# Turning the quantized inputs by transposing DMA transfers in nine of the first eleven batches

## What is computed

```python
r_t = 0.9 * r_(t-1) + ctx_t * ctx_t              # a scan over the 512 rows of a batch
x = x + layernorm(x) * r
y = layernorm(x)
xq, s1 = quant_act_uint8(y)                      # one scale, from the maximum over all 32 batches
h = relu(xq @ quant(w1).T + b1)                  # 512 -> 2048
hq, s2 = quant_act_uint8(h)                      # again one scale over everything
x = x + (hq @ quant(w2).T + b2)                  # 2048 -> 512
```

## Time and profile before

| | |
|---|---|
| median of 3 runs | 1227.15 us (1222.93 to 1229.25) |
| the profiled execution, its own time | 1226.19 us |
| its span (first to last instruction) | 1224.0 us |
| TensorE busy | 1150.7 us, 94% |
| ScalarE busy | 950.9 us, 78% |
| VectorE busy | 870.7 us, 71% |
| moved by DMA | 448.72 MB, mean 367 GB/s |
| mean granted clock of TensorE | 0.978 of full |

### The profile page before, as it was taken

The page is one execution under the profiler, slowest core; times in us unless marked ns, Lnnn a source line. Parts: engine busy times, 40 slices in busy tenths (PEclk is TensorE's granted clock), DMA queues, the critical chain, the costliest instruction groups (busy, mean ns, idle before and its releaser), DMA issues.

```text
span 1224.0 us, 14776 instructions
## 1 busy us (share of the span) xinstructions
PE 1150.7 (94%) x5194; PEld 524.1 (43%) x5194; DVE 870.7 (71%) x1273; ACT 950.9 (78%) x1191; POOL 153.0 (13%) x400
## 2 busy tenths in 40 slices
PE   6888988886999999999999999899999999999998
PEld 2333333323444555444444444344444444444443
DVE  6999889985777897777777777555565555655565
ACT  5888978995777777777777775788888888888784
POOL 4455645551000110000000000000000000000000
PEclk9899889997999999999999999899999999999999
DMA  9999999922778999999999978799999999999996
GB/s 391 395 401 398 386 385 401 405 100 104 313 292 322 400 425 414 377 356 359 351 352 354 354 325 334 300 349 416 424 424 423 423 424 425 422 424 423 424 424 248
DMA packets 63570, 448.72 MB, mean 367 GB/s; under 512 B 6900, under 2 KB 6920, under 8 KB 9480
## 3 DMA queue, kind: packets, MB, share of 16 engines
q1 hardware_dynamic: 51976, 363.89, 72.7%
q10 hardware_dynamic: 11520, 83.89, 18.4%
HBM read 254.81 MB, written 192.94 MB: 366 GB/s over the span
## 4 chain that ended last, share of the span: by engine, by line
PE 79%; DMA 7%; ACT 6%; DVE 4%; issue 3%; POOL 1%; SPq 0%; ACTq 0%; DVEq 0%; POOLq 0%
PE ps L929 36%; PE ps L975 36%; DMA xq<-in_ctx_dram 6%; PE ps L901 3%; ACT xq L536 2%; PE ps L951 2%; ACT xq L525 2%; PE ps L893 1%; DVE work L680 1%; ACT xq L533 1%; DVE work L696 1%; DMA xq<-in_x_dram 1%; DVE xq L690 0%; ACT work L533 0%; ACT w1T L542 0%
## 5 line engine op out<-in xcount | busy, mean ns | idle before, releaser
L929 PE MATMUL ps<-xq,w1T 128*128 128x512 f16 x2048 | 449.5, 380 | 1.4 <-DVE xq L777 1.4
L975 PE MATMUL ps<-w2T,xq 128*128 128x512 f16 x2048 | 445.2, 380 | 2.3 <-ACT xq L638 2.0
L768 DVE TENSOR_REDUCE work<-xq 128x2 f32<-128x1024 f32 x255 | 309.8, 1219 | 116.6 <-ACT xq L582 116.6
L638 ACT ACTIVATE xq<-xq,hb,hs 128x512 f16<-128x512 f32 x446 | 321.0, 801 | 67.9 <-PE ps L975 58.9
L582 ACT ACTIVATE xq<-ps 128x1024 f32<-128x1024 f32 x255 | 260.9, 1023 | 126.9 <-PE ps L929 126.7
L975 PEld LDWEIGHTS ps<-w2T,xq 128*128 128x128 f16 x2048 | 200.7, 98 | 246.8 <-ACT xq L638 4.4
L929 PEld LDWEIGHTS ps<-xq,w1T 128*128 128x128 f16 x2048 | 199.3, 98 | 236.0 <-issue 2.1
L824 DVE TENSOR_TENSOR work<-ps,cs_bc 128x512 f32<-128x512 f32 x128 | 88.4, 692 | 183.0 <-PE ps L975 176.2
L893 PE MATMUL ps<-xq,work 128*128 128x512 f32 x256 | 140.2, 634 | 35.5 <-ACT xq L525 35.1
L901 PE MATMUL ps<-xq,work 128*128 128x512 f32 x192 | 107.3, 642 | 13.3 <-ACT xq L536 12.9
L536 ACT ACTIVATE xq<-ps,ones,cs_bc 128x512 f32<-128x512 f32 x128 | 98.9, 772 | 10.8 <-PE ps L901 9.5
(11 more groups left out here) (112 smaller groups left out, 511.4 us busy)
## 6 DMA issues: line engine op xcount, KB each, us to landing
hidden_scratch<-xq SPq DMA_DIRECT2D x120, 1024.0 KB, 6.9
xq<-hidden_scratch SPq DMA_DIRECT2D x104, 1024.0 KB, 26.6
work<-x_scratch ACTq DMA_DIRECT2D x42, 1024.0 KB, 10.5
xq<-in_ctx_dram SPq DMA_DIRECT2D x32, 1024.0 KB, 9.2
xq<-in_x_dram SPq DMA_DIRECT2D x24, 1024.0 KB, 10.4
x_scratch<-xq SPq DMA_DIRECT2D x24, 1024.0 KB, 8.6
out_dram<-work ACTq DMA_DIRECT2D x24, 1024.0 KB, 9.0
w1T<-hidden_scratch SPq DMA_DIRECT2D x16, 1024.0 KB, 27.1
```

Of the source, the lines that this page charges most:

```text
L638: act.activation(hq[c % HQ], src[:, c % 2, :], ACT.Relu, bias=hb[:, q:q + 1], scale=hs[:, q:q + 1]).then_inc(h_scaled, 1)
L768: dve.tensor_reduce(hmax[:, b * NF + 2 * q:b * NF + 2 * q + 2], src, AX.X, ALU.max).then_inc(kept_maxed, 1)
L929: last = pe.matmul(bank, w1T[:, k, f * P:(f + 1) * P], xq_rows(b, k), start=(k == 0), stop=(k == KD - 1))
L975: last = pe.matmul(acc_bank(s, i), src[:, i * P:(i + 1) * P], w2T[:, q, :], start=first, stop=final)
```

## The change

In batches 2 to 10 of the second stage (`moved`) TensorE's 16 transposes and VectorE's copy are left out. SP issues four transposing DMA transfers per batch in their place, one for each tile i, from the quantized rows in SBUF to the slot in `xq`, also in SBUF; each moves 128 x 512 float16. They are issued at the end of batch b for batch b + 2, after a wait for the last quantized tile and for the last product of batch b, and ahead of that iteration's `load_w2`. The slots of turned rows go from three to two, and the quantized rows get a second buffer in the space of the third. The waits are counted anew: TensorE's first product of a moved batch waits for the transfers, and so does ScalarE's `quantize` where it writes over their source; the waits for turned batches count only the batches that TensorE still turns; and the use of the two shared PSUM banks by w2 and x is ordered by waits on `w_kept`.

```diff
-NXQ = 3
+NXQ = 2
...
+    moved = list(range(2, 11))
+    NW2 = 4
...
-        qi = work[:, 2 * ROW:2 * ROW + ROW // 2].bitcast(F16).rearrange("p (i d) -> p i d", i=NI)
+        qi = [work[:, 2 * ROW:2 * ROW + ROW // 2].bitcast(F16), xq[:, NXQ * KD * S:(NXQ + 1) * KD * S]]
...
-        o = NXQ * KD * S // 2
+        o = (NXQ + 1) * KD * S // 2
...
+        x_moved = [sem(f"x_moved{n}") for n in range(2)]
...
+        def turns_before(b):
+            return len([t for t in range(b) if t not in moved])
+        def moves_until(b):
+            return NI * len([t for t in moved if t <= b and t % 2 == b % 2])
+        def w2_turns_before(b):
+            return min(max(b - W2_AT - 3, 0), NW2)
...
                     sp.dma_start(h_dram[n, q // 2], doubles[c // 2 % NFIRST]).then_inc(h_stored[c // 2 % NFIRST], 16)
+                if b + 2 in moved:
+                    sp.wait_ge(x_scaled, (b + 3) * NI)
+                    sp.wait_ge(hid_ready, (b + 1) * NP2)
+                    at = xq_slot(b + 2) * (KD * S)
+                    for i in range(NI):
+                        into = xq[:, at:at + KD * S].rearrange("p (k s) -> p k s", k=KD)[:, :, i * P:(i + 1) * P]
+                        sp.dma_start_transpose(into, qi[b % 2][:, i * D:(i + 1) * D]).then_inc(x_moved[b % 2], 16)
                 if 0 <= b - W2_AT < NQ:
                     load_w2(b - W2_AT)
...
-                    wait_count(act, x_turned, t)
-                act.activation(qi[:, i, :], quantized_from(t)[:, i, :], ACT.Relu, bias=qb[:, u:u + 1],
+                    if t - 2 in moved:
+                        act.wait_ge(x_moved[t % 2], 16 * moves_until(t - 2))
+                    else:
+                        wait_count(act, x_turned, turns_before(t - 1))
+                act.activation(qi[t % 2][:, i * D:(i + 1) * D], quantized_from(t)[:, i, :], ACT.Relu, bias=qb[:, u:u + 1],
...
-                dve.wait_ge(x_turned, b + 1)
+                dve.wait_ge(x_turned, turns_before(b + 1))
...
-                    if q == 2 and b + 1 < NB:
+                    if q == 2 and b + 1 < NB and b + 1 not in moved:
                         keep_xq(b + 1)
...
-                pe.wait_ge(xq_kept, b + 2)
+                pe.wait_ge(xq_kept, turns_before(b + 2))
+                pe.wait_ge(w_kept, 2 * NQ + k)
...
-                if q == 0:
-                    pe.wait_ge(xq_kept, b + 1)
+                if q == 0 and b in moved:
+                    pe.wait_ge(x_moved[b % 2], 16 * moves_until(b))
+                elif q == 0:
+                    pe.wait_ge(xq_kept, turns_before(b + 1))
...
-                wait_count(pe, xq_kept, b)
+                wait_count(pe, xq_kept, turns_before(b))
+                pe.wait_ge(w_kept, 2 * NQ + w2_turns_before(b - 1))
...
-                    if q == 2 and b + 1 < NB:
-                        if 0 <= b - 1 - W2_AT - 3 < NQ:
-                            pe.wait_ge(w_kept, 2 * NQ + b - 1 - W2_AT - 2)
+                    if q == 2 and b + 1 < NB and b + 1 not in moved:
                         turn_x(b + 1)
...
+            pe.wait_ge(w_kept, 3 * NQ)
             spread(2)
```

More of the change, by code:

```diff
@@ L950, in turn_x @@
                     for k in range(KD):
-                        last = pe.transpose(tp_banks[:, k * S + i * P:k * S + (i + 1) * P], qi[:, i, k * P:(k + 1) * P], ident_b[:, :])
+                        last = pe.transpose(tp_banks[:, k * S + i * P:k * S + (i + 1) * P], qi[b % 2][:, i * D + k * P:i * D + (k + 1) * P], ident_b[:, :])
                 last.then_inc(x_turned, 1)
```

## The result

The changed kernel takes 1241.43 us (median of 4 runs, 1239.43 to 1242.77) against 1226.79 for the kernel before beside it: 1.012 times as long, 95% interval 1.0098 to 1.0141. The forecast was 1229.5 in a range of 1218 to 1252. A second measurement gave 1.0136 (1.0113 to 1.0159).

What follows compares the result with a forecast made beforehand. TensorE alone was taken to set the second stage's pace: -8.1 us of transposes, +8.6 of waits and +1.8 of clock loss gave +2.3, moving the median from 1227.15 to about 1229.5 us. The range was 1218 to 1252 us.

Steps and rivals of the forecast that it cites:

- B: Rival: four transfers above 3.4 us overfill the engines from batch 2 on, the queue grows; 1251 or 1276 us; chance 0.30.
- C: Rival: SP needs 3 us per transposing issue, 2 us wait in each of batches 2 to 8; 1241.7 us; chance 0.05.
- B's named case: Four transfers cost 5.5 us, batches 2 to 6 take 15.9 us, the clock falls twice: +24 us, 1251 us.
- the pieces without a gap: Profile sign: the chain's pieces in batches 2 to 8 stand 13.8 us apart, not 14.7.
- the 368 transposes: Profile sign: 368 transposes remain at line turn_x, 512 less 144.
- The saving: Second stage: nine batches lose 16 transposes each on TensorE, 9 x 0.90 = 8.1 us; VectorE's nine copies save nothing.
- X, the price of four transfers: DMA engines' time per batch of four transposing transfers: 2.5 us, twice the lower end 1.24; share 0.93 in batches 2 to 6.
- Batch 8, no wait: Transfers issued at 395.0, store ahead landing at 399.3, plus 2.5 us, against batch 7's end at 407: no wait.
- Batches 9 and 10, 2.7 and 5.9 us: TensorE waits for late transfers at the starts of these batches, together 1.1 + 3X = 8.6 us.
- The clock: A TensorE wait may drop the granted clock, 1.8 us each time; counted once, with 0 to 3.5 us as bound.
- The ring of hidden stores: ScalarE's reuse of store places: slowest store lands after 25.2 us against 27.1 allowed, no wait, by 1.9 us.
- SP issues in 0.32 us: SP's queue: each transposing issue priced like a plain transfer's 0.32 us, 1.3 us more per batch with 2.8 us free.

Runs made afterwards that it cites:

- experiment 5: The changed kernel with the four loads of w2 moved from batches 5 to 8 to batches 12 to 15: 1238.69 us, 1.0098 of the kernel before.
- experiment 4: The changed kernel with plain copies in place of the transposing transfers, rows left unturned in batches 2 to 10: 1233.39 us, 1.0048 of the kernel before.
- experiment 1: The changed kernel with only batches 2 to 7 turned by transfers, 8 to 10 back on TensorE: 1224.41 us, 0.9983 of the kernel before.
- experiment 7: The changed kernel with w2 loads from batch 12 on and x2 loads issued in SP's queue: 1230.94 us, 1.0036 of the kernel before.

## Why the prediction was right or wrong

The range holds the result, and slower by over 0.5% had the largest of the three chances, 0.43. The forecast itself, 1229.5, was 12 us short. Between 1223 and 1235 I had put 0.45, and the result fell where rivals B and C lay. The range held it because it took in B's named case, not because the forecast's own sum was near. Of the signs in the profile, the pieces without a gap and the 368 transposes came; the waits were three and not two, and the share in batches 3 to 6 was 1.03 and not 0.93.

- *The saving.* 9 x 0.90 = 8.1 us, and VectorE's copies free: right, the 432 matmuls without a gap show it.
- *X, the price of four transfers.* The step that failed first, and not by the figure itself: 2.5 us is what four of them took by themselves, in batch 2. The prediction took the same price for transfers between 1 MB stores, and there it was 3.7 to 4.1. Doubling the lower end for 2-byte columns was luck: a plain copy in runs of 256 bytes, which turns nothing, takes as much. The Trainium skill has two figures ("DMA: Bandwidth & Descriptors", Latency and other measured facts, and "Advanced Engine Details and Errata", X-Bar Transpose): 261 GB/s, and "as fast as regular". The trace has 0.51 MB in 2.5 us of the engines, 206 GB/s, by themselves, where plain copies of the same runs have 219, so the second agrees for copies of that kind; beside the stores, at 128 to 142 GB/s, neither does.
- *Batch 8, no wait.* Wrong, 5.2 us. X above 3.4 was B's condition, and it was met: the engines had no time left in batches 3 to 7, and the first load of w2, issued at 387.77, found a full queue. A transfer of batch 8, issued at 391.8, landed after 15.8 us (shown with SP's queue above), where the earlier trace rows had 5.0 for the store ahead. With w2 moved away (experiment 5) the wait was 2.2, and with plain copies (experiment 4) there was none.
- *Batches 9 and 10, 2.7 and 5.9 us.* 6.2 and 4.2 measured; the sum of 1.1 + 3X is 13.4 with X = 4.1 (12.2 with 3.7), and all three waits are 15.7. The sum was near in total, for the plain copies too; its split over the batches was not.
- *The clock.* Counted once at 1.8 us with 3.5 as the bound; all three waits brought it, 6.9 us in all. I took the price from 16 matmuls after a long idle stretch, which gave 1.8 us; behind the waits it was 2.6, 2.7 and 1.7. The second term that was mis-sized, mostly in its count.
- *The ring of hidden stores.* No wait in the changed kernel, as predicted. That the margin was thin is shown by experiment 1, where TensorE's own waits no longer gave the queue time.
- *SP issues in 0.32 us.* Wrong by far: 1.27 us at least, 2.3 in the middle, 11.9 at most. Rival C had this mechanism and, at 3 us an issue, 1241.7 us. That this is so near the result is luck: it wanted a wait of 2 us in every batch with idle engines beside it, and there was none in batches 2 to 7, where the engines were full.
- *B as named* took X = 5.5 and 1251 us. It had the engines filled from the first moved batches on, which is what made batch 8 late. But the queue did not grow from batch to batch, and SP's long issues, C's part, were on the path from 391.8 us on. Neither rival alone is what happened.

Put together: +2.3 forecast, with 7.1 us more of waits (15.7 in place of 8.6) and 5.1 more of clock (6.9 in place of 1.8), is +14.5.

## What to carry to other kernels

A transfer with a deadline must be priced against the queue in front of it at that moment, read from what the landings of its neighbours take, and with its own load added to every later one. Its price must be taken beside the transfers that it will run with: by itself it cost 2.5 us here, between stores 3.7 to 4.1. Moving work from a full engine to the DMA paid here only where the DMA engines had time to spare both then and in the stretch that inherits the backlog: six batches and a later w2 gave 0.54%, nine batches cost 1.2%. Before a run, ask what an issue does to the queue that issues it, since whatever stands behind it comes in a burst.

## What the runs showed of the hardware that I had not expected

- A transposing transfer of 128 x 512 float16 within SBUF shows as some 544 small packets (19584 more under 512 B on the page than before, for 36 transfers). Four take all 16 engines for 2.5 us when they run by themselves, and 3.7 to 4.1 us between 1 MB stores of the same queue. Plain copies of the same bytes in 256-byte runs take 2.4 to 2.5 us in both places, not the 1.24 that long rows would.
- Its issue held SP for 1.27 us in three of batch 2's four, with one store ahead or none, and for up to 11.9 us behind a full one; one of 128 x 2048 held it for 30. Four plain copies in 256-byte runs held it for up to 15.6 us in all.
- Beside packets of another queue it slows down and so do they, and the engines read as busy by over 1 while they move little: 1.24 at 133 GB/s, 1.31 at 105. With one queue for all the sign is weaker (1.21 at 255 GB/s) but not gone. One queue removed 13 us of waits in experiment 7 against 5. Why, no run here tells.
